# Delta rule of a two-layer model on one core: `dout` in the turn of `du`, both halves of `uw` in one turn, order tables redrawn

## The reference, cut to what matters

```python
u = T @ v_c
wm = T @ kb_c
def step(S, xs):
    q_i, k_i, u_i, w_i, wm_i = xs
    u_i = (u_i - wm_i @ S) * w_i[..., None]
    a = jnp.where(causal, q_i @ jnp.swapaxes(k_i, -1, -2), 0.0)
    o_i = q_i @ S + a @ u_i
    return (S + jnp.swapaxes(k_i, -1, -2) @ u_i, o_i)
```

## Time and profile before

| | |
|---|---|
| median of 3 runs | 1239.53 us (1236.46 to 1243.86) |
| the profiled execution's own time | 1239.64 us |
| its span | 1238.2 us |
| mean granted clock of TensorE | 0.985 of full |
| busy: PE / DVE / ACT / POOL | 1161.1 / 913.7 / 707.2 / 840.4 us |
| waits of TensorE from 0 to 175 us, the largest | POOL's `prob` 5.8 us in 4 |
| DMA | 230.87 MB, mean 186 GB/s |

### The profile page before, as it was taken

The page is one execution under the profiler, slowest core; times in us unless marked ns, Lnnn a source line. Parts: engine busy times, 40 slices in busy tenths (PEclk is TensorE's granted clock), DMA queues, the critical chain, the costliest instruction groups (busy, mean ns, idle before and its releaser), DMA issues.

```text
span 1238.2 us, 31062 instructions
## 1 busy us (share of the span) xinstructions
PE 1161.1 (94%) x11890; PEld 922.5 (75%) x11890; DVE 913.7 (74%) x1902; ACT 707.2 (57%) x2020; POOL 840.4 (68%) x1156
## 2 busy tenths in 40 slices
PE   5887789999999999999999999999999999899998
PEld 3454458877778788787887877987788877788786
DVE  4958786986888978885687787986677766784534
ACT  5787877656756564467645665457775533332322
POOL 3745467687688845799488726798669736873871
PEclk9889989999999999999999999999999999999999
DMA  7101165654366665773477556685257666777763
GB/s 267 35 23 52 33 225 183 211 193 157 117 192 206 208 198 172 250 253 115 168 234 242 180 165 197 230 280 165 94 161 228 227 205 242 237 249 250 262 225 125
DMA packets 91186, 230.87 MB, mean 186 GB/s; under 512 B 9888, under 2 KB 16160, under 8 KB 90912
## 3 DMA queue, kind: packets, MB, share of 16 engines
q1 hardware_dynamic: 90896, 228.30, 56.3%
q10 hardware_dynamic: 144, 0.59, 0.1%
HBM read 225.71 MB, written 3.15 MB: 185 GB/s over the span
## 4 chain that ended last, share of the span: by engine, by line
PE 57%; DVE 22%; ACT 10%; issue 4%; DMA 3%; POOL 2%; DVEq 0%; SPq 0%; ACTq 0%; POOLq 0%
PE bank L948 13%; PE bank L901 12%; PE bank L612 5%; PE bank L829 4%; DVE ogate L1358 4%; PE bank L938 3%; PE bank L919 3%; DVE dy L1211 2%; PE bank L647 2%; PE bank L929 2%; DMA kv<-values 2%; DVE kv L1125 2%; PE bank L671 2%; ACT prob L1469 2%; PE bank L657 1%
## 5 line engine op out<-in xcount | busy, mean ns | idle before, releaser
L1744 POOL TENSOR_TENSOR vgate<-vgate,xT 128x512 f32<-128x512 f32 x256 | 325.7, 1298 | 72.0 <-DMA vgate<-gates 67.3
L901 PE MATMUL bank<-wv,vgate 128*128 128x128 f32 x2048 | 252.6, 277 | 1.6 <-POOL vgate L1744 1.0
L901 PEld LDWEIGHTS bank<-wv,vgate 128*128 128x128 f32 x2048 | 242.4, 192 | 13.4 <-issue 7.8
L948 PE MATMUL bank<-ogate,wo 128*128 128x256 f32 x1024 | 242.7, 383 | 2.1 <-DVE ogate L1358 1.7
L948 PEld LDWEIGHTS bank<-ogate,wo 128*128 128x128 f32 x1024 | 188.5, 190 | 33.0 <-issue 8.9
L1358 DVE TENSOR_TENSOR ogate<-ogate,bank 128x1024 f32<-128x1024 f32 x128 | 153.4, 1212 | 34.6 <-PE bank L938 28.3
L1469 ACT ACTIVATE prob<-prob,mx 128x128 f32<-128x128 f32 (+1 forms) x256 | 96.0, 377 | 47.6 <-DVE mx L1061 47.2
L1628 ACT ACTIVATE mprob<-bank,mmin 128x256 f32<-128x256 f32 x128 | 59.4, 469 | 107.5 <-DVE mmin L1347 106.9
L1676 POOL TENSOR_TENSOR rot<-rot 128x512 f32<-128x512 f32 x64 | 82.0, 1281 | 55.2 <-DVE rot L1037 54.9
L612 PE MATMUL bank<-wqkv,hT 128*128 128x512 f32 x192 | 107.0, 661 | 2.9 <-ACT hT L1405 1.9
L1721 POOL TENSOR_TENSOR dlt<-dlt,step 128x126 f32<-128x126 f32 (+22 forms) x248 | 93.3, 376 | 19.4
(11 more groups left out here) (224 smaller groups left out, 2385.5 us busy)
## 6 DMA issues: line engine op xcount, KB each, us to landing
ogate<-gates SPq DMA_DIRECT2D x128, 512.0 KB, 4.2
vgate<-gates SPq DMA_DIRECT2D x128, 512.0 KB, 4.0
wo<-in_wo_moe SPq DMA_DIRECT2D x128, 256.0 KB, 4.6
wv<-in_wv_moe SPq DMA_DIRECT2D x128, 256.0 KB, 4.5
kv<-values SPq DMA_DIRECT2D x64, 256.0 KB, 4.7
local<-in_local SPq DMA_DIRECT2D x1, 1715.0 KB, 9.4
wqkv<-in_wqkv SPq DMA_DIRECT2D x2, 768.0 KB, 6.4
x<-in_x SPq DMA_DIRECT2D x8, 128.0 KB, 5.3
```

Of the source, the lines that this page charges most:

```text
L901: i = nc.tensor.matmul(out[:, n * D:(n + 1) * D], xg[:, e, n * P:(n + 1) * P], m.wv[slot][:, e, :], start=(q, n, e) == (0, 0, 0), stop=(q, ...
L948: i = nc.tensor.matmul(out[:, 0:T], m.wo[slot][:, e, :], cg[:, e, :], start=(h, q, e) == (0, 0, 0), stop=(h, q, e) == (MH - 1, 1, EQ - 1))
L1744: i = tt(gate[:, e:e + half, :], gate[:, e:e + half, :], spread(m.xT[b % 2][:, :], 1, half), ALU.mult)
```

## The change

`uw` fills both its banks in one turn on TensorE and empties both in one turn on VectorE; `dout` of the chunk before is called at the end of `du`; the bank `delta_sum` is taken in `du` of chunk 1, ahead of the bank of `du`, and no longer in `dout`; all strings of turns and the string of banks are drawn anew. The number of operations and their sizes stay the same. TensorE has 1258 turns instead of 1322, VectorE 1289 instead of 1297; ScalarE, POOL and SyncE keep 914, 584 and 351.

```diff
 SCALAR_TURNS = (
-    "GaaaaaGGGaaaaaGaaaaaXababbabbbabbababbabaaaacaacbGcaabaGcbaaGabbbaabbbaaaababGGaabGbaaacabcbGbcbbbcbbabbabaaca"
+    "GaaaaaGGGaaaaaGaaaaabaaXbbabbbabbababbaabaaacaacbcaabacbaaGGabbbaabbbaaaababGaabbGGGaaacabcbGbcbbbcbbabbabaaca"
...
-    ticks += [[("dT", b)], [("uw", b, 0)], [("uw", b, 1)], [("st0", b)]]
+    ticks += [[("dT", b)], [("uw", b)], [("st0", b)]]
     for c in range(NC_):
-        ticks += [[("du", b, c)] + ([("dout", b, c - 1)] if c else []), []]
-        if c < NC_ - 1:
-            ticks += [[("ds", b, c)], []]
+        ticks += [[("du", b, c)]] + ([[("ds", b, c)]] if c < NC_ - 1 else [])
     return ticks + [[("dout", b, NC_ - 1)], [("dres", b)], [("drms", b)], [("dwo", b)]]
...
-KEPT = [("gla_sum", "gsum", (0,)), ("delta_sum", "dout", (0,)), ("moe_sum", "mproj", (0, 0)), ("values", "hv", (0,)),
+KEPT = [("gla_sum", "gsum", (0,)), ("delta_sum", "du", (1,)), ("moe_sum", "mproj", (0, 0)), ("values", "hv", (0,)),
...
-    def uw(b, a):
-        bank = banks.of("uw", b, a)
-        out = split(take(bank), n=NC_)
-        pe.wait_ge(s.vkc, nth("dstart", b))
-        pe.wait_ge(s.winvT, nth("dT", b))
-        for c in range(NC_):
-            i = per_head(out[:, c, :], m.winvT[:, a * NC_ + c, :], flat(m.vkC[:, c, :, :]), start=True, stop=True)
-        i.then_inc(bank.filled, 1)
+    def uw(b):
+        for a in range(2):
+            bank = banks.of("uw", b, i=a)
+            out = split(take(bank), n=NC_)
+            pe.wait_ge(s.vkc, nth("dstart", b))
+            pe.wait_ge(s.winvT, nth("dT", b))
+            for c in range(NC_):
+                i = per_head(out[:, c, :], m.winvT[:, a * NC_ + c, :], flat(m.vkC[:, c, :, :]), start=True, stop=True)
+            i.then_inc(bank.filled, 1)
 
     def du(b, c):
+        if c == 1:
+            take(banks.kept("delta_sum", b))
         bank = banks.of("du", b, c)
...
         i.then_inc(bank.filled, 1)
+        if c:
+            dout(b, c - 1)
 
     def dout(b, c):
         bank = banks.kept("delta_sum", b)
-        out = take(bank)[:, c * CH:(c + 1) * CH]
+        out = bank.ap[:, c * CH:(c + 1) * CH]
```

More of the change, by code:

```diff
@@ new lines @@
+    "APDVDVADAVDADPPDADVADAVDADPDPDADVAADVADPPDAADPPE")
+VECTOR_TURNS = (
+    "VaaaaaaaGaaaaabGGbbaGGbbGGbGGbaabaaGGGGaacGGcbcaabbGGbccccbGaabbaabaaGbaabbGcGcbbcGGbGbGGbGGcccGcGGGaaGcaacGGc"
+    "GaaGabcccaacbbzCGabbCGbaaCCACACCCCaaCFaaGFbaaabFGbFabbGGcbGGGGVFVaaOAOAcacaGGFVVcccOOAcAzCbCVVbaaOAbAOabaCCCFF"
+    "bVFVGbbcGGbCCcGcAGGAbVCVCbGbCbVVODDOGDcccFFOAOAVFcVcFOcOAcaAaaaGOOAaAaDcccDDVVcOOGFFAbAaabbGFbDFDbDGFDbaaGGDaa"
+    "DVGVGDGDbDODObGDGGAVVaAaDDaDaGGDGGGGGcbGVcbbcDVbADADbVVDDbEbDObcccaGaOcOzCAOACaaGVVaaCCCCCOAOAFVFFVCOOAFAaaVCC"
+    "VaaFODOAFVVAGDDDcDbDcbbDGcObGGGOAcccDGAFFcbFDGGDbOzDCObGCDGbADDAVVDCCDCCcCDOcDOcCVVACDFDFDAFcVVccCFDDGEGDFFOOF"
+    "AcaAFaFVGVGOGOAGAaaGGaaVVOOAAaaOaAaOAVbVbbDOObDADAaabVaabbVaabDaaDVVDDDGbDbcbDOcbOcADAVVDcccDGcDbDDbbDGODbOAAV"
+    "DVDDGaaDDGaDcGGcGcAaGAGVVGGOOaacccOOAAGGGGGGVVGGEOAOAcazCaCOaGOAGVVAbObbDAObaVGADVDbbaaVOVOaAaCCbACFbCCCDFCCcF"
+    "cDAOVVFcAOaacccbDcDbbDzCDObCDFDAOADVVDaDaDFDFDFCCDCFCDCDCDACVADbDVObbCbDOVGAOVOAGFcGFVGcGVFcGGGGOAOAFEVVccccFO"
+    "OaAaAVVGGGGOOAaAGaGGaaGVVDOOAAaaVVDDababbDOOAbDADGVDVbDbbaabDDaDaFDDDaDaDOODbcDbGbcDFbFDADcaAFaGDDEcccDVVbcbbO"
+    "OGbGaaGAaaGAGGVVGcGGaacOcOAAcccVVacaOzOCAbCAVVbbbOOAAVVCCCODOAbACCbCDVVCbOObFFAFACDVGGFcVGDGGcDGODODAcGDAGDFDV"
+    "VDFDOODAAVDVGDGccDcFDFFDGDODVVDOAcAzCDDCDEOVVAOACCCCCOVOVAFAFCFOOCACAFVVFFOFFDOVAFVADDDDODVODVADADDDDODOVDVADA"
+    "DDDDDODOADDAVVDEOOAVVAOOAAVVOOAAODAOADDDVDVODOVDVADADDODOVDVADADDDOODVADADDDOOE")
@@ new lines @@
+GPSIMD_TURNS = (
+    "aaaaaaaabGbGbGGabaaaGGaaGabaGbabaabaaGaababbGGbGGGaGaaaGaGaababGbaaaaaaabaWbWbGGGWaaWaWaGWWWbWaaabaWbWbGGGWWbb"
+    "WDGWDDDDDDaaaDaDaWWWWGaababDDDDbWaDaGDaDWDaGDDbDGWGaDDaWDaaGDGGWbGWbWDWbDDDDDWWDaaWWDaaWaDabaaGDDWDbWDbWGDGDGD"
+    "bDDWbDDGDDWDWDWWWDGDDDDDWWaaaDaDWaaaWaDbWGbWWaaaabGabDaGaDaWDDWDWbDDbDWDWDGDDDbDDbWWaDaaDDGDGGGaaDWWGGDGaGDWaW"
+    "aDGDbWWbWWbaWaaabDDaaWDWDDWDbDbDWDDaDWDDaDDWWDWbbWDDDWGWDGWWDGGDWWGDaaDWaaGWGaGWaaWabDbDDDWDbWbDaDaDaDaDDDaDaD"
+    "DbGbaaDDWbDbDaaaWaDWaWDWaDWaaWDGGWGbDbGWWbWbGDGDGDWDWDWDDGDDWWDWDWWDGDDDWWWDWWDDDDDDDWWDWWWWDDDWDDDWDDDDWDDDWD"
+    "DWDWDDDDDDDDWWWDDWDDWDWDDDDWDDDDDD")
@@ L137 @@
+    "GGvoooovovvvvvGGGGooExovvCoovoovvooovovvovvovvovvGGGGGoovvvoooGGGGoovvEoxovovovovooGGGGGoCovvvovvovvvovoCvvooo"
+    "vvoEoxGGvvoGGovvoovvoovvooGoGGGGoEvvvvoovvovvooovvoovooGGGGCovvvoovvvvvovovvvvooEooooovvvoCovovvovvoovvoovvooE"
+    "oovoovvoooovvvoovoooE")
 BANK_TURNS = (
[L138 to L139 removed]
@@ L145 @@
[L145 to L148 removed]
+    "76543210765204375625607625430276530246327453627427656423175643725613456174526751430517254730265702437650243765"
@@ L1281, in dT, with uw @@
         nc.vector.transpose(m.winvT[:, :, :].rearrange("p g i -> p i g"), flat(m.solved)).then_inc(s.winvT, 1)
-    def uw(b, half):
-        bank = banks.of("uw", b, half)
+    def uw(b):
         v.wait_ge(s.dw, nth("dgates", b))
-        rows = m.uw[:, half * NC_:(half + 1) * NC_, :, :].rearrange("p c a t -> p c (a t)")
-        tt(rows, chunks(filled(bank)), spread(m.gates[b % 2][:, 2 + half, :], 2, 2 * CH), ALU.mult).then_inc(bank.emptied, 1)
+        for half in range(2):
+            bank = banks.of("uw", b, i=half)
+            rows = m.uw[:, half * NC_:(half + 1) * NC_, :, :].rearrange("p c a t -> p c (a t)")
+            tt(rows, chunks(filled(bank)), spread(m.gates[b % 2][:, 2 + half, :], 2, 2 * CH), ALU.mult).then_inc(bank.emptied, 1)
     def st0(b):
         for a in range(2):
-            bank = banks.of("uw", b, a)
+            bank = banks.of("uw", b, i=a)
             v.wait_ge(bank.emptied, bank.use)
```

86 lines of the change are left out of this document (31 added, 55 removed).

## The result

The changed kernel takes **1234.96 us** (median of 17 runs, 1230.33 to 1240.19), the kernel before 1241.8 us (17 runs beside them): ratio 0.9948, 95% interval 0.9931 to 0.9966. I had forecast 1237.5 in a range of 1228 to 1248, made against 1239.6 for before, a ratio of 0.9983. The range held; the gain is 6.5 us by the ratio where I had summed 2.1. At 0.52% it lies a hair outside the class within 0.5% that held my forecast, and the interval covers both sides of that line. The profiled executions differ by 6.4 us in span (1238.2 and 1231.8) and can be laid side by side.

A forecast was written before the change was run, and what follows sets the result against it. TensorE's own list was taken to bound the kernel from 775 to 930 us, a chain through all engines its start. 1239.6 - 2.0 - 1.9 + 1.2 + 0.6 gave 1237.5 us, range 1228 to 1248.

The forecast's parts named there:

- Fewer passages: On TensorE, 150 groups of 32x32 tiles become 144, each giving back 0.33 us: 2.0 us less, down to 1.2.
- The start: VectorE's second gated-attention pair and ScalarE's `w_qk` copy move behind the first softmax's work: 1.9 us less, bounded by 0.
- Banks: The new bank table has more close reuse, 32 instead of 21 takes under 1.0 us: 1.2 us more, 0 to 2.5.
- Two `uw` banks: Two banks in one `uw` turn add nothing, as other turns lie between VectorE's multiplications and the first `du`.
- The tail: Last `dout` moves ahead of last `mpT`, the delta rule's end ahead of the last `ogate`: 0.6 us more, 0 to 1.3.
- No arithmetic is removed: Operations keep number and size on all engines; moved turns of POOL and SyncE were priced at nothing.
- The signs: If right: some 144 groups, first 64x128 probabilities transpose near 31 us, TensorE waits near 30 us, last `mproj` pair unbroken.
- Absorbed: Rival: other limits, such as POOL's waits for gated loads, take the gain, leaving 1239.6 us; chance 0.15.
- The start gains by the clock: Rival: two half-clock stretches at the start get full speed, 8.4 us less, 1229.1; chance 0.26, shared with better hiding.
- Pinned `dout`: Rival: `dout` in `du`'s turn halts TensorE for POOL's `dlt_sum`, 10 us, 1247.5; chance 0.22, shared with worse hiding.

The follow-up runs named there:

- the old ends in the new order: Changed kernel with start and tail in the order of before, the middle untouched: 1235.22 us, ratio 0.9966 to the kernel before.
- the fold alone: Kernel before with `dout` always at the end of `du` and both `uw` in one turn, all other order kept: 1260.2 us, ratio 1.0145.
- the five profiles above: Profiles of the changed kernel, its version with start and tail as before, and three with tiny matmuls added: 19.1 to 25.9 us of waits for others.
- the best of four tries: Changed kernel with 46 tiny matmuls spread over three places where TensorE idles: 1232.22 us, ratio 0.9923 to the kernel before.
- the padded before: Kernel before with tiny matmuls put in front of TensorE's first transpose; with 26 of them 1249.02 us, ratio 1.0076.
- the version with `dout` apart: Changed kernel with each of the 56 inner `dout` one turn later than `du`, in its own turn: 1241.45 us, ratio 1.0006 to the kernel before.

## Why the prediction was right, and where its terms were off

**Fewer passages** (2.0 less, down to 1.2). The mechanism held, the size was the lower half: 0.24 us a group as measured on 30 others, so 6 x 0.24 = 1.4 us. The shortfall against 0.33 fits what I had allowed for at the lower bound, gains that a wait behind them swallows; the profiles show fewer waits where there are more passages, but not place by place.

**The start** (1.9 less). The first `probT` starts at 31.33 instead of 32.88, 1.5 earlier, and the old ends in the new order cost 2.2 us although their tail saves 0.4, so 2.6 for the start. That agrees, but the intervals don't resolve it, and between the profiles of before and after only 0.8 of the 1.5 is left at 178 us. In single profiles the start says little: the fold alone, with the order of before there, was 3.8 us ahead of before at 208 us, with half-clock stretches at other places.

**Banks** (1.2 more, 0 to 2.5). The trace shows it directly: a turn held by its bank starts 0.04 us after the bank's last user signals. That is so for 21 of 1042 takes before and 26 of 1034 after, and TensorE lost 10.8 and 13.6 us there: 2.8 more. Counted as TensorE's idle time alone it is 8.2 and 10.5, 2.3 more. The term was mis-sized by about two, at or above its upper bound. My need of 0.9 to 1.2 us is for an eviction that starts at once, and its 0.3 us of signals stood on no row: the traces show 0.02 from the filled bank's signal to an eviction that has its engine free. Most of the evictions behind these waits did not start at once: at 185.9 us the copy of `probT` began 0.7 us after the bank was full, at 150.5 us one of `rot` 10.3 us after.

**Two `uw` banks** (0). Right for this order. In the timeline of VectorE after the change, image 7 again:

```profile
1178.68 1.51 DVE L1290 TENSOR_TENSOR uw<-bank,gates 128x512 f32<-128x512 f32 x2 [0.63 <-PE bank L826]
1180.30 0.71 DVE L1296 STREAM_TRANSPOSE winvT<-uw 128x512 f32<-128x512 f32 x1
...
1182.15 0.22 DVE L1305 TENSOR_TENSOR dlt<-uw,bank 128x64 f32<-128x64 f32 x1 [1.01 <-PE bank L826]
```

VectorE is done with the preparation at 1181.1 and itself waits 1.01 us for the first `du`. But my reason was incomplete: I read it from a pair that the old order had covered. The other pairs of the old order, merged without a redraw, cost 5 us. The rule of the Trainium skill, "TensorEngine Tiling (Array Packing)", Performance Considerations, that emptying PSUM may become the bound behind small tiles, gave 5.5 us by my working. No run shows such a cost in the order of the change. The merged `uw` in the old order shows it in part: 1.6 of its 5 us are a wait for a bank of `uw`, 1.6 for the work behind it, the rest isn't put down to it.

**The tail** (0.6 more, 0 to 1.3). Measured 0.43, and the working held: the first `ogate` starts 3.36 after `mpT`, where I had worked out 3.33. The timeline of TensorE after, with the one row of VectorE from that of all engines, to be read against the earlier trace rows:

```profile
1219.93 0.26 PE L826 MATMUL bank<-state_sum,dy 32*32 32x32 f32 x8
...
1220.18 0.66 PE L931 MATMUL bank<-small,mprob 128*128 128x128 f32 x4
1221.78 1.10 PE L940 MATMUL bank<-mprobT,vmoe 128*128 128x256 f32 x4 [0.94 <-issue]
1223.54 2.31 DVE L1361 TENSOR_TENSOR ogate<-ogate,bank 128x1024 f32<-128x1024 f32 x2
1223.67 0.70 PE L883 MATMUL bank<-dsq,layer 128*128 128x256 f32 x2 [0.79 <-DVE dsq L1332]
1224.87 3.69 PE L950 MATMUL bank<-ogate,wo 128*128 128x256 f32 x16 [0.50 <-DVE ogate L1361]
```

The last pair is unbroken, as said, and starts 4.69 us after `mpT` (3.88 before).

**What the sum left out** is the step that failed: "No arithmetic is removed ... I put nothing on these moves". The redraw moved several hundred turns in the middle, and TensorE waits 10.3 us less for others from 175 us on (3.5 to 10.3 by the five profiles above; the waits for banks are part of them). I had those 30 us in view and put a better covered middle into a rival's chance only. The terms as measured (1.4 + 1.5 less, 2.3 to 2.8 and 0.4 more) come to nearly nothing, -0.2 to +0.3; it is the middle that makes the kernel faster, less what the stops take. So the number fell into the range, and on the side that I had named, by luck as far as the sum goes.

**The signs** that I had named came mixed: 144 groups, the first `probT` at 31.33 and the last `mproj` pair unbroken are there. TensorE's waits from 175 us on are 25.6 us and not near 30, and one of the signs of being wrong is there too, a new wait of several us in the saturated part that no term holds: the stop of 2.77 us.

**The rivals.** *Absorbed* is refuted by the ratio. *The start gains by the clock*: no. In the stretches up to 175 us the granted clock is 0.50 for 37.5 us before and 41.0 after. They were exchanged, as I had said against it:

```profile
30.80:41.00 10.20, 9.40 (x62) 5.13 (x62) 9.79 (x22) 7.39 (x27) 6.69 (x7) 0.50 0.01 2
129.80:140.00 10.20, 8.68 (x31) 4.24 (x32) 5.04 (x17) 8.98 (x34) 2.81 (x3) 0.50 0.00 1
```

*Pinned `dout`*: the mechanism is real and I had its price almost right (10 us; 10.8 measured in waits, 13 in time), but it belongs to the fold in the old order. In the new one it takes 0.6 us in two waits. My evidence for it, that more of POOL's `du` and `ds` turns stand behind a gate, did not tell the two orders apart. What I take to count instead, and did not test by itself, is how far behind `du` of the chunk before TensorE comes to the turn.

## What to carry to other kernels

A merge of two turns and the order around it are one change: the fold cost 18 us in the old order, while in the new one its `dout` alone is worth 7 us. When every table is redrawn, do not price the moves at nothing because the work is the same; take the sum of the bottleneck's waits as the stake, and say which part of it a better order can take. And a stop that a profile shows at one place, however clear its cause, is worth what its removal measures in the median. Here that was 3 us in the best of four tries, not told apart from nothing, where the trace promised 5 and more.

## What the runs showed of the hardware that was not expected

- TensorE can run out of instructions. Its queue for instructions brings 16 KB for 256 of them; a fetch lands some 1 us after it starts, and TensorE goes on 1.3 to 1.6 us after the landing if it has reached the block's end by then. In all profiles the block ends lie behind number 193 of 256, counted from the first recorded instruction, so instructions put in front shift them along the program. A `uw` of 256 instructions in 1.92 us is fast enough for that, at 0.8 to 3.0 us a stop in the change. That it costs time in executions that aren't profiled isn't shown.
- Matmuls of 2 columns on 32x32 tiles were dearer than those of 64 columns: 92 MATMULs took 5.06 us at 6 us (0.055 each), 36 took 1.29 at 17 us and 28 took 1.04 at 29 us (0.036), while `uw` runs 128 in 1.92 later (0.015). What makes the difference, the place or the size, wasn't tried.
- A wait of TensorE in the saturated part can be paid in part twice. Behind the stop at 557 us the granted clock was 0.50 for 3.4 us, as it was at the stop of 2.73 us in the padded before; in the wait at 331 to 336 us it fell at 333 and stayed there for 6.8 us. Behind the stops of 2.62 and 2.25 us in two other profiles it did not fall, and at waits of 1.1 us for `mprob` and 0.75 for `mprobT`, near 1080 us, it fell for 3.4 us in the version with `dout` apart and not in the change. So the length of one wait doesn't settle it.
